# Operands of the bias and selector matmuls allocated on 33 or 40 partitions instead of 128

## What is computed

```
x += tanh(g0) * xattn(layernorm(x), ctx)   # diagonal self attention (a linear map and a bias),
                                           # LN, 8-head cross attention on 77 keys + out bias,
                                           # LN, FFN 256-1024-256 with biases, LN
x += tanh(g1) * moe(layernorm(x))          # 2 shared experts and 8 routed ones (top 2), SwiGLU
x += tanh(g2) * xattn2(layernorm(x), ctx)  # softmax over the 1024 tokens
x += tanh(g3) * rwkv_ffn(layernorm(x))     # token shift, sigmoid gate, relu squared
```

## Time and profile before

| | |
|---|---|
| median of 2 runs | 596.36 us (596.23 to 596.48) |
| the profiled execution | 596.48 us |
| its span, first to last instruction | 594.7 us |
| mean granted clock of TensorE in it | 0.932 of 2.4 GHz |
| PE busy | 495.1 us, 83% |

### The profile page before, as it was taken

The page is one execution under the profiler, slowest core; times in us unless marked ns, Lnnn a source line. Parts: engine busy times, 40 slices in busy tenths (PEclk is TensorE's granted clock), DMA queues, the critical chain, the costliest instruction groups (busy, mean ns, idle before and its releaser), DMA issues. The chain is left out here.

```text
span 594.7 us, 9657 instructions
## 1 busy us (share of the span) xinstructions
PE 495.1 (83%) x2948; PEld 431.5 (73%) x2948; DVE 395.0 (66%) x891; ACT 226.7 (38%) x580; POOL 193.3 (33%) x257
## 2 busy tenths in 40 slices
PE   3957889999879879796997999999999995377765
PEld 3546878889768768686876888888888873267654
DVE  1855387777743848667489587567667666887564
ACT  1445677777636434343421311111121111434432
POOL 5532464555537334344214020000000000335453
PEclk9979699999999989898999999999999996678798
DMA  8800000000002210202000000000000000000012
GB/s 247 286 2 1 1 2 1 0 0 0 2 3 87 68 50 1 88 0 62 28 0 28 2 0 2 1 0 0 0 0 0 0 0 0 2 0 19 18 36 71
DMA packets 13762, 16.42 MB, mean 28 GB/s; under 512 B 1698, under 2 KB 11939, under 8 KB 13604
## 3 DMA queue, kind: packets, MB, share of 16 engines
q1 hardware_dynamic: 13172, 15.38, 8.1%
q10 hardware_dynamic: 560, 0.67, 0.4%
HBM read 13.95 MB, written 2.10 MB: 27 GB/s over the span
## 5 line engine op out<-in xcount | busy, mean ns | idle before, releaser
L1509 POOL TENSOR_TENSOR rstd<-var,half 128x4 f32<-128x4 f32 (+2 forms) x36 | 33.5, 930 | 212.1 <-DVE var L94 166.8
L938 ACT ACTIVATE work<-PS 128x512 f32<-128x512 f32 x40 | 23.9, 598 | 111.5 <-PE PS L83 107.6
L81 PE MATMUL PS<-XT_hi,GU_hi 128*128 (+1 forms) x160 | 64.4, 403 | 0.0
L82 PE MATMUL PS<-XT_lo,GU_hi 128*128 (+1 forms) x160 | 63.2, 395 | 0.0
L83 PE MATMUL PS<-XT_hi,GU_lo 128*128 (+1 forms) x160 | 63.1, 394 | 0.0
L1355 DVE TENSOR_TENSOR work<-PS,work 128x512 f32<-128x512 f32 x40 | 27.6, 690 | 42.6 <-PE PS L83 42.2
L81 PE MATMUL PS<-DN_hi,hid_hi 128*128 128x256 f32 x160 | 45.5, 284 | 6.2 <-DVE hid_lo L1364 4.8
L1231 DVE TENSOR_TENSOR hid_lo<-work,hid_hi 128x512 fp32r<-128x512 f32 x32 | 25.7, 804 | 33.7 <-ACT hid_hi L866 33.7
L83 PE MATMUL PS<-DN_hi,hid_lo 128*128 128x256 f32 x160 | 44.6, 279 | 0.0
L82 PE MATMUL PS<-DN_lo,hid_hi 128*128 128x256 f32 x160 | 44.5, 278 | 0.0
L799 ACT ACTIVATE Pm<-PS,mx 128x77 f32<-128x77 f32 x128 | 39.8, 322 | 4.1 <-issue 2.1
(11 more groups left out here) (314 smaller groups left out, 1524.0 us busy)
## 6 DMA issues: line engine op xcount, KB each, us to landing
moe_raw<-gu SPq DMA_DIRECT2D x20, 128.0 KB, 2.8
rawA<-raw SPq DMA_DIRECT2D x4, 512.0 KB, 8.7
xr<-x SPq DMA_DIRECT2D x4, 512.0 KB, 3.7
out<-X SPq DMA_DIRECT2D x8, 256.0 KB, 2.1
X<-x SPq DMA_DIRECT2D x1, 1536.0 KB, 12.7
moe_raw<-dn SPq DMA_DIRECT2D x10, 128.0 KB, 2.7
w1raw<-w SPq DMA_DIRECT2D x1, 1024.0 KB, 8.5
w2raw<-w SPq DMA_DIRECT2D x1, 1024.0 KB, 10.1
```

What stands on the lines that cost most here:

```text
L81: pe.matmul(o, a[0], b[0], start=first, stop=False, skip_group_check=skip)
L82: pe.matmul(o, a[0], b[1], start=False, stop=False, skip_group_check=skip)
L938: act.activation(work[q][:, :], PS[:, CG + q, :], ACT.Silu).then_inc(c_s, 1)
L1509: return pool.tensor_tensor(rstd[:, k:k + n], var[:, k:k + n], half[:, 0:n], ALU.pow)
```

## The change

The partition dimension of seven tensors goes from 128 to the highest row in use plus one: `b2row`, `ones`, `bias` and `sbias` to 33, `cT`, `sel` and `selraw` to 40. Free dimensions, data and all instructions stay in place; each instruction that names such a tensor whole now covers 33 or 40 partitions or rows.

```diff
-        b2row = sb(top, "b2row", [P, D], F32R)
+        b2row = sb(top, "b2row", [33, D], F32R)
...
-        ones = sb(top, "ones", [P, P], F32R)
+        ones = sb(top, "ones", [33, P], F32R)
...
-            bias = sb(stage_a, "bias", [P, 2 * D], F32R)
-            sbias = sb(stage_a, "sbias", [P, B, 2, HM], F32R)
+            bias = sb(stage_a, "bias", [33, 2 * D], F32R)
+            sbias = sb(stage_a, "sbias", [33, B, 2, HM], F32R)
...
-            cT = sb(stage_c, "cT", [P, CH], F32R)
+            cT = sb(stage_c, "cT", [LO_ROW + E, CH], F32R)
...
-            sel = sb(stage_c, "sel", [P, E, P], F32R)
-            selraw = sb(stage_c, "selraw", [P, E, P])
+            sel = sb(stage_c, "sel", [LO_ROW + E, E, P], F32R)
+            selraw = sb(stage_c, "selraw", [LO_ROW + E, E, P])
```

## The result

The changed kernel takes 628.45 us (626.15 to 630.76, 2 runs) against 596.36 us, a ratio of 1.054 with an interval of 1.038 to 1.071. Timed again beside three other kernels (the run after_again) it takes 626.43 us against 597.46 us, ratio 1.047 (1.042 to 1.052). So it is slower by 27 to 32 us. Three of the medians in this document hold one run that took over 1.5% longer than the fastest of its kernel; without it they are 624.81 us for after_again, 611.54 for bias_only and 624.45 for sel_twice. The profiled execution has a span of 624.1 us, 29.4 us more than before.

A forecast was written before the change was run, and what follows sets the result against it. PE's stream was taken to bound stages A and C. Stage C 9.0, stage A 5.2 + 1.7 + 1.0 and stage B 1.1 sum to 18.0 us on 596.48, giving 614.5 us, range 595.5 to 634 us.

The forecast's parts named there:

- the case of no cost: Rival: PE overlaps both kinds of matmul in rows as in columns, 0 us a switch; 596.4 us, chance 0.36.
- The likeliest case: Middling drain at each switch, 0.10 to 0.20 us; 614.5 us, own range 607.5 to 625 us, chance 0.40.
- The price of a switch: PE going between matmuls of 128 rows and 33 or 40, or back, stalls 0.14 us; 224 times in all.
- the uncovered load: PE's weight load not hidden behind the previous matmul, read at a restart after a wait: 0.11 us.
- the lost overlap: Time a PE matmul is still under way while its successor already streams, lost at a switch: 0.17 us.
- The full drain: Rival: PE finishes the last matmul, then loads weights, 0.28 us a switch; sum 41.9 us, 638 us, chance 0.12.
- Stage C: 32 selectors, 64 switches at 0.14 us with PE always late and no cover: 9.0 us.
- Stage A's steps: Ten steady steps, 81.3 to 149.7 us: 8 switches, 1.12 us less 0.6 slack, 0.52 us each, 5.2 us.
- The first steps: Stage A, 33 to 75 us, lower clock: only switches ahead of DVE's statistics count, 4 x 3 x 0.14 = 1.7 us.
- The last steps: Stage A, 155 to 170 us: only line 462 left, half of it covered, 1.0 us.
- Stage B: First 4 biases uncovered, 1.1 us; the loop's 12 hide in normalized-tile waits, which shrink about 1 us each.
- POOL: Clearing of the constants and making of sel, whether shorter or longer, are covered: 0 us.

The follow-up runs named there:

- bias_only: Changed kernel with cT, sel and selraw back on 128 partitions, so only ones, bias, sbias and b2row stay on 33: 613.66 us, ratio 1.032.
- sel_twice: Changed kernel with each selector matmul issued twice in a row: 625.86 us, ratio 1.047.
- the fill runs: Kernel before and changed kernel, each with 14 matmuls of 512 columns ahead of each of stage B's three normalized-tile waits: 590.83 us and 622.40 us.
- cols32: Kernel before with one more matmul of 128 rows and 32 output partitions ahead of each selector: 603.11 us, ratio 1.012.

## Why the prediction was right, and where it was off

The forecast was slower by 18.0 us through stalls at the switches, with 628.45 inside the range of 595.5 to 634. That range was made wide to hold the case of no cost and says little. The likeliest case's own range ended at 625 us, and the measured time lies above it. The stall at each switch, its main places and its sign held; the size of the main term did not, and neither did the reason given for the stall.

- The price of a switch was taken as 0.14 us, the middle between the uncovered load (0.11) and the lost overlap (0.17). It is 0.195. The step that failed is the choice of a middle where the two follow each other: the load does wait, in full, and the lost overlap comes on top of it, but with 0.09 instead of 0.17, because the load may start shortly before the recorded end of the matmul in flight. The full drain's mechanism was the nearest, with its first part counted twice too large. By the sum's own working at 0.20 a switch the loss is 28.2 us, and 27 to 32 were measured. That this comes so near is in part luck: stages A and C lost less than their terms, and the other three places as much or more, as follows.
- The reason for the stall was that a short matmul could overtake a long one ahead of it. The runs speak against it: 65 rows are fewer than 128 too and do not stall, and leaving the short kind, where nothing could be overtaken, costs as much as entering it.
- Stage C was put at 64 switches with no cover, 9.0 us; at 0.20 it would be 12.8. Measured from the first to the last selector it is 10.6, and with the outer two switches 11.0: that is the 28 pairs of 0.40 us less 0.3. The first four selectors had cover, as PE waits beside each of them in the kernel before. The waits of the earlier trace rows were read as a small sum, and not as lying just there.
- Stage A's steps: 10 steps were to grow by 5.2 us. From the y bias at 81.3 to that at 149.7 us they took 68.4 us; the same ten take 74.5 now, 6.1 more. Two errors nearly cancel. A step's 8 switches cost 1.50 us by the starts in the step at 126.64 us (0.38, 0.39, 0.39 and 0.34 a pair), not 1.12. And its slack was larger than 0.6: the step at 123.10 us had 0.60 us of gap before line 81 plus 0.10 for the load uncovered there, and every second step had the 0.25 us shown above and some 0.1 us more gap on top. The steady steps went from 6.69 to 7.36 us. That the wait for PT_lo would go was right.
- The first steps were put at 1.7 us. They cost 2.4 us in after_again and 6.9 in the profile shown. The stretch's low clock was read in the earlier trace rows but a change of it was not thought of; no rival held that. Whether the stalls bring it about is not shown for this stretch.
- The last steps, 1.0 us: 2.7 us were lost from the last y bias to the last line 462 (21.7 against 19.0). At a clock of 1.00 it is 1.2 (20.3 us in bias_only), near the term, and by some luck: the term was for line 462 alone, from 155 us on, while the earlier trace rows has a score bias as late as 156.9, and the step between 149.7 and 155 us has no term. The other 1.4 us go with the lower clock, which was not thought of here either.
- Stage B, 1.1 us: 2.8 in the profile, 2.1 between the fill runs, which leave out most of the stage's own spread. So of the 16 biases' stalls (6.4 us at 0.40 a pair) most do disappear in waits. The wait for the normalized tile went from 11.9 to 10.6 us, 0.4 for each of the three; the forecast was 1 us for each.
- POOL, at nothing: the clearing of `sbias` on 33 partitions and the making of `sel` on 40 take as long as on 128 (no difference of more than 0.01 us in the rows of both traces), and both are covered.

On the rule weighed in the prediction: the Trainium skill, TensorEngine Tiling (Array Packing), Key Properties, says that a change of tiling mode drains TensorE. For rows the traces agree that each switch stalls, with 0.195 us a switch and the limit between 64 and 65 rows, which is also where its Performance Considerations put row tiling. For columns they show no such stall: cols32 has none with 32 output columns; whether PE takes that for another mode no run tells. The rival of no cost rested on carrying over the columns to the rows; the columns were measured rightly (transposes with all 128 output partitions show the same starts as those of the earlier trace rows, 0.35 and 0.32 us apart at 441.55 us of the changed kernel) and do not speak for the rows.

What stays open: what exactly is waited for in the 0.09 us (no run separates the array from the queue), and why executions of one kernel differ by up to 10 us in total, with stage B between 131 and 141 us over the kernels without filling, and two lengths of the first and of the last steps with short matmuls.

## What to carry to other kernels

Where matmuls of 128 rows follow each other in a dense stream, one of 32 to 64 rows among them cost 0.34 to 0.40 us of PE's time on top of its own here, about half going in and half coming out, with 256, 308 or 512 columns alike. With zero rows up to 128 this cost is gone, and with 65 rows too but for 0.02 us a selector. If short ones are needed, put them side by side. A wait next to the short one can hide the cost. Look at the starts of neighbours in PE's order and at whether the load begins one matmul early: busy shares and the other engines' waits would not have told the cause.

## What the runs showed that was not expected

A short matmul's weight load is recorded a little shorter (a median of 182 to 183 ns for 32 to 64 rows, 188 for 65 and 128) and is still the dearer one, since it is not started ahead. The selector with 65 rows is recorded with 400 ns where 128 rows have 388, and the 28 selectors take 0.59 us from predecessor to third matmul where they took 0.57, for which no run here gives a reason. And a wait of 3 to 4 us in the middle of a dense stage costs more than itself here: filling three of them with 14 useless matmuls each made the kernel before 5.3 us faster, 4.7 of it in stage B of the profiles, whose granted clock was 1.00 instead of 0.95.
